# Fixed sets of PSUM banks for the feed-forward matmuls in place of a running count over seven banks

## The chip, the cores and the metric

The kernel runs on all eight cores of one Trainium2 chip. Each core runs the same program on its own four sequences of the batch and exchanges nothing with the others. The metric is the device time of the slowest core in microseconds (us).

## What is computed

The input x has 32 sequences of 2048 tokens with 1024 features. Three blocks follow one another, each on a layer norm of its input and each added to it: half of a gated feed-forward block, an attention-like block with a decaying running sum, and half of the same feed-forward block again.

```python
def ffn(x, w_gate, w_up, w_down):        # weights are int32, times 1/127
    gate = x @ (w_gate / 127).T          # 1024 -> 3072
    up   = x @ (w_up / 127).T            # 1024 -> 3072
    return (silu(gate) * up) @ (w_down / 127).T

x = x + 0.5 * ffn(layernorm(x), w_gate, w_up, w_down)
x = x + attn(layernorm(x), Wq, Wv, Wo, Wg, beta, ln_gamma, ln_beta)
x = x + 0.5 * ffn(layernorm(x), w_gate, w_up, w_down)
```

In `attn`, q, v and a gate are projections of x, the state is a running sum of v with one decay per head, q times the state is normalised, multiplied by silu of the gate, and projected with Wo.

## The kernel before, in words

**Order of the program.** The weights are first cast and transposed into scratch tensors in HBM (`prep_cast`, `prep_T_gu` L396 on, `prep_T_d`). Then, for each of the four sequences s = 0 to 3, come phase A (`ffn_phase`), phase B (`attn_phase`) and phase C (`ffn_phase` again). The attention weights are transposed by DMAs that the SyncE queue (SP) issues during the first phase A (`prep_T_attn`).

**A small scheduler.** The class `Em` records the instructions of each engine in the order of the code and works out the semaphore waits from names of resources. It never reorders anything. Each PSUM bank is one such name (`PSB0` to `PSB6`). `group` records the eight matmuls that accumulate into one bank; the first of them waits until whoever last read that bank is done. So the order of work is the order of the code, and which earlier read a matmul waits for is set by the bank number alone.

**PSUM.** `PSB[0]` to `PSB[6]` are seven banks of 128x512 fp32; an eighth, `PSB7`, holds transposes.

**`ffn_phase`.** It begins with a layer norm (`layer_norm_to_xn`): for each of 16 chunks of 128 tokens, VectorE normalises (L566), TensorE transposes eight 128x128 blocks into PSB7 (L570), ScalarE copies them to XN (L576). The hidden dimension of 3072 is worked in three slabs j = 0, 1, 2 of 1024. In each slab there are five passes over TensorE, one after the other:

- gate, first half (hs = 0): 16 groups of 8 matmuls (L610), each group read out of its bank by ScalarE with Silu into SG (L627);
- up, first half: 16 groups (L638), each read out by VectorE, which multiplies by SG into H (L648);
- gate, second half, and up, second half, in the same way (hs = 1);
- down: 32 groups (L664), two for each chunk c of 128 tokens, read out in slab 0 by ScalarE (L674) and in slabs 1 and 2 by VectorE, which adds them to ACC (L678).

In slab 2, after the two groups of a chunk, VectorE adds ACC to X (L684). In phase A it then also sums the chunk for the next layer norm (`ln_stats`, L541, with a square on ScalarE, L545).

**The tail of phase C.** There `boundary_cb` is called for each chunk. After chunks 3, 7, 11 and 15 it stores a quarter of X (L911) and loads the same quarter of the next sequence over it (L916), both on the GpSimd queue (POOL). After chunks 7, 11 and 15 it also puts the four sums (L541) of the quarter loaded before into VectorE's queue, which wait for that load. The last quarter's sums come behind the phase.

**Banks.** One counter `pbc` runs through all passes of a phase, and each group takes the next of seven banks. In phase B the three projections of a chunk (`proj`, L722) take banks 4, 5 and 6 in turn and are read out by ScalarE (L735, L744, L749).

```python
bank = pbc[0] % 7        # in each of the three passes
pbc[0] += 1
```

Of the kernel before, what the change touches and what calls it, by code (L numbers as in the profile page):

```python
# [246 lines left out]
def build_program():  # L247
# [331 lines left out]
    def ffn_phase(tap=False, prestats=True, next_stats=True, tail_cb=None,  # L579
                  skip_gw0=False):  # L580
        layer_norm_to_xn(prestats=prestats)
        if tap:
            em.dma("st", lambda g: g.dma_start(out=dbg_xn, in_=XN[:]),
                   reads=[k for row in kXN for k in row], writes=["DBGXN"])
        nsl = NSLAB if DBG_SLABS is None else DBG_SLABS
        pbc = [0]
        for j in range(nsl):
            li = 3 * j
            slots = [(WA, "WSLOTA"), (WB, "WSLOTB")]
            wg_sl, wg_k = slots[li % 2]  # L590
            wu_sl, wu_k = slots[(li + 1) % 2]
            wd_sl, wd_k = slots[(li + 2) % 2]
            if not (skip_gw0 and j == 0):
                em.dma("wl", lambda s, a=wg_sl, j=j: s.dma_start(
                    out=a[:].rearrange("p (k h) -> p k h", h=SLAB), in_=scr_g[:, j]),
                    reads=[f"scrT_wgate_r{r}" for r in range(HID // 128)], writes=[wg_k])
                em.dma("wl", lambda s, a=wu_sl, j=j: s.dma_start(
                    out=a[:].rearrange("p (k h) -> p k h", h=SLAB), in_=scr_u[:, j]),
                    reads=[f"scrT_wup_r{r}" for r in range(HID // 128)], writes=[wu_k])
            if tap and j == 0:  # L600
                em.dma("st", lambda g, a=wg_sl: g.dma_start(out=dbg_wa, in_=a[:]),
                       reads=[wg_k], writes=["DBGWA"])
            for hs in range(2):
                for g in range(4):
                    for m4 in range(4):
                        m = 4 * hs + m4
                        bank = pbc[0] % 7
                        pbc[0] += 1
                        items = [(lambda t, k=k, m=m, g=g, wg_sl=wg_sl, bank=bank:
                                  t.matmul(PSB[bank][:],  # L610
                                           wg_sl[:, SLAB * k + 128 * m:SLAB * k + 128 * (m + 1)],
                                           XN[:, S * k + 512 * g:S * k + 512 * (g + 1)],
                                           start=(k == 0), stop=(k == KC - 1)),
                                  [wg_k] + [kXN[k][4 * g + i] for i in range(4)])
                                 for k in range(KC)]
                        em.group("tensor", items, writes=[kPSB[bank]])
                        if tap and j == 0 and hs == 0 and g == 0 and m4 == 0:
                            dps = HF[:, 4096:4608]
                            em.op("vector", lambda v, bank=bank: v.tensor_copy(
                                dps, PSB[bank][:]),  # L620
                                reads=[kPSB[bank]],
                                writes=[kH[4][i] for i in range(4)], war=B_H)
                            em.dma("st", lambda g2: g2.dma_start(out=dbg_ps, in_=dps),
                                   reads=[kH[4][0]], writes=["DBGPS"])
                        dst = SG[:, S * m4 + 512 * g:S * m4 + 512 * (g + 1)]
                        em.op("scalar", lambda s, dst=dst, bank=bank:
                              s.activation(dst, PSB[bank][:], AF.Silu,  # L627
                                           scale=np32(1.0 / 127.0)),
                              reads=[kPSB[bank]], writes=[kSG[m4][g]],
                              war=["WGT"] + PREP_SG_KEYS)  # L630
                for g in range(4):
                    for m4 in range(4):
                        m = 4 * hs + m4
                        hc = m
                        bank = pbc[0] % 7
                        pbc[0] += 1
                        items = [(lambda t, k=k, m=m, g=g, wu_sl=wu_sl, bank=bank:
                                  t.matmul(PSB[bank][:],  # L638
                                           wu_sl[:, SLAB * k + 128 * m:SLAB * k + 128 * (m + 1)],
                                           XN[:, S * k + 512 * g:S * k + 512 * (g + 1)],  # L640
                                           start=(k == 0), stop=(k == KC - 1)),
                                  [wu_k] + [kXN[k][4 * g + i] for i in range(4)])
                                 for k in range(KC)]
                        em.group("tensor", items, writes=[kPSB[bank]])
                        dst = H[:, S * hc + 512 * g:S * hc + 512 * (g + 1)]
                        src0 = SG[:, S * m4 + 512 * g:S * m4 + 512 * (g + 1)]
                        em.op("vector", lambda v, dst=dst, src0=src0, bank=bank:
                              v.tensor_tensor(dst, src0, PSB[bank][:], ALU.mult),  # L648
                              reads=[kSG[m4][g], kPSB[bank]], writes=[kH[hc][g]],
                              war=B_H)  # L650
            if tap and j == 0:
                em.dma("st", lambda g: g.dma_start(out=dbg_sg, in_=SG[:]),
                       reads=ALL_SG, writes=["DBGSG"])
                em.dma("st", lambda g: g.dma_start(out=dbg_h, in_=H[:]),
                       reads=ALL_H, writes=["DBGH"])
            em.dma("wl", lambda s, a=wd_sl, j=j: s.dma_start(
                out=a[:].rearrange("p (k h) -> p k h", h=D), in_=scr_d[:, j]),
                reads=[f"scrT_wdown_s{j}r{r}" for r in range(D // 128)], writes=[wd_k])
            for c in range(NCH):
                for n in range(2):  # L660
                    bank = pbc[0] % 7
                    pbc[0] += 1
                    items = [(lambda t, hc=hc, c=c, n=n, wd_sl=wd_sl, bank=bank:
                              t.matmul(PSB[bank][:],  # L664
                                       H[:, S * hc + 128 * c:S * hc + 128 * (c + 1)],
                                       wd_sl[:, D * hc + 512 * n:D * hc + 512 * (n + 1)],
                                       start=(hc == 0), stop=(hc == 7)),
                              [wd_k, kH[hc][c // 4]])
                             for hc in range(8)]
                    em.group("tensor", items, writes=[kPSB[bank]])  # L670
                    dst = ACC[:, D * c + 512 * n:D * c + 512 * (n + 1)]
                    if j == 0:
                        em.op("scalar", lambda s, dst=dst, bank=bank:
                              s.activation(dst, PSB[bank][:], AF.Copy, scale=SFIN),  # L674
                              reads=[kPSB[bank]], writes=[kACC[c][n]], war=WAR_ACC_A)
                    else:
                        em.op("vector", lambda v, dst=dst, bank=bank:
                              v.scalar_tensor_tensor(dst, PSB[bank][:], SFIN, dst,  # L678
                                                     ALU.mult, ALU.add),
                              reads=[kPSB[bank], kACC[c][n]], writes=[kACC[c][n]])  # L680
                if j == NSLAB - 1 or (DBG_SLABS is not None and j == DBG_SLABS - 1):
                    xc = X[:, D * c:D * (c + 1)]
                    ac = ACC[:, D * c:D * (c + 1)]
                    em.op("vector", lambda v, xc=xc, ac=ac: v.tensor_tensor(  # L684
                        xc, xc, ac, ALU.add),
                        reads=[kX[c], kACC[c][0], kACC[c][1]], writes=[kX[c]])
                    if next_stats:
                        ln_stats(c)
                    if tail_cb is not None:
                        tail_cb(c)  # L690
        if tap:
            em.dma("st", lambda g: g.dma_start(out=dbg_acc, in_=ACC[:]),
                   reads=ALL_ACC, writes=["DBGACC"])
# [289 lines left out]
```

How the kernel before makes its waits and increments, by code:

```python
        def body(engobj, eng):  # L225
            waited = {}
            for inst in em.ins[eng]:
                for dep in inst["deps"]:
                    sem, val = resolve(dep)
                    key = id(sem)
                    if waited.get(key, 0) < val:
                        engobj.wait_ge(sem, val)
                        waited[key] = val
                bi = inst["fn"](engobj)
                if inst["stream"] is not None:
                    bi.then_inc(semh[("d", inst["stream"])], 16)
                elif inst["inc"]:
                    bi.then_inc(semh[("e", eng)], 1)
```

## Time and profile before

| | us |
|---|---|
| Time, median of two runs | 7798.15 |
| The two runs | 7376.51 and 8219.79 |
| The profiled execution: its own time | 7241.5 |
| Its span (slowest core, core 1) | 7240.0 |
| Shortest span of a core (core 2) | 7209.6 |
| PE busy (share of the span) | 5696.3 (79%) |
| DVE busy | 2079.6 (29%) |
| ACT busy | 1474.6 (20%) |
| POOL busy | 173.1 (2%) |

PE is TensorE's matmuls, PEld its weight loads, DVE VectorE, ACT ScalarE, POOL GpSimd and SP SyncE. A matmul's row lasts from its start to its modelled end. Matmuls overlap in the pipeline, so the distance from one start to the next is shorter than a row. "Idle before" is the idle time of an engine ahead of an instruction, and the arrow names what ended it. PEclk is the granted clock of TensorE as a share of full speed.

### The profile page before, as it was taken

What the parts mean: (1) busy time and instruction counts of PE and PEld (TensorE: products, weight loads), DVE (VectorE), ACT (ScalarE), POOL (GpSimd) and SP (SyncE); (2) the same over time, 40 slices, a digit from 0 to 9 for tenths busy, and PEclk for the clock granted to TensorE, in tenths of its full rate; (3) what the DMA queues carried; (4) which work ended last, traced back from release to release, by engine and by line L of the source; (5) the groups of instructions that cost most, each with busy time, mean ns of one, the idle gap of its engine ahead of it and who ended that gap; (6) DMA issues with size and microseconds to landing.
All of it is one profiled execution on the core that took longest, in us unless ns stands there. A gap on an engine that the chain in (4) does not pass through costs nothing.

```text
span 7240.0 us, 81303 instructions; the slowest of 8 cores (7209.6 to 7240.0 us)
## 1 busy us (share of the span) xinstructions
PE 5696.3 (79%) x29138; PEld 2832.0 (39%) x29138; DVE 2079.6 (29%) x3929; ACT 1474.6 (20%) x2342; POOL 173.1 (2%) x112
## 2 busy tenths in 40 slices
PE   1012999686998799786998799786999799786899
PEld 0011444343443344443443344443444344443444
DVE  0012124244123213344123213444123213444123
ACT  1000212222211211322211221322211221322211
POOL 0000000000000000000000000000000000000000
PEclk9999999787999899887999899887999799887999
DMA  8733013200013000100013110100013110100001
GB/s 99 116 95 98 24 47 78 75 1 24 24 47 98 31 36 24 47 1 24 24 47 84 40 40 24 47 1 24 24 38 86 41 47 24 47 1 24 24 36 70
DMA packets 152527, 322.14 MB, mean 44 GB/s; under 512 B 112336, under 2 KB 112336, under 8 KB 140048
## 3 DMA queue, kind: packets, MB, share of 16 engines
q1 hardware_dynamic: 134016, 239.10, 10.0%
q0 software_dynamic: 18128, 77.84, 6.3%
q8 instruction: 253, 4.15, 0.2%
q14 instruction: 130, 1.06, 0.1%
HBM read 291.74 MB, written 88.08 MB: 52 GB/s over the span
## 4 chain that ended last, share of the span: by engine, by line
PE 70%; DVE 9%; DMA 8%; issue 5%; ACT 4%; another core or an unknown queue 3%; DVEq 1%; SPq 0%; ACTq 0%; POOL 0%; POOLq 0%
PE PSB L610 19%; PE PSB L638 18%; PE PSB L664 14%; PE PSB L722 9%; PE PSB L850 5%; PE PSB7b L570 2%; ACT XN L576 2%; DMA TSTB<-nat_g 2%; DMA o<-X 1%; DVE ACC L678 1%; DMA TSTB<-nat_u 1%; DVE STATS L541 1%; ACT ACC L843 1%; PE PSB7b L839 1%
## 5 line engine op out<-in xcount | busy, mean ns | idle before, releaser
L648 DVE TENSOR_TENSOR H<-SG,PSB 128x512 bf16<-128x512 bf16 x768 | 527.7, 687 | 2621.4 <-PE PSB L638 2621.4
L627 ACT ACTIVATE SG<-PSB 128x512 bf16<-128x512 f32 x768 | 458.5, 597 | 2200.7 <-PE PSB L610 2200.7
L610 PE MATMUL PSB<-XN,WA 128*128 128x512 bf16 x4096 | 902.9, 383 | 0.0
L664 PE MATMUL PSB<-WA,H 128*128 128x512 bf16 x4096 | 888.6, 379 | 6.7 <-DVE ACC L678 6.7
L638 PE MATMUL PSB<-XN,WB 128*128 128x512 bf16 x4096 | 889.3, 379 | 0.0
L610 PEld LDWEIGHTS PSB<-XN,WA 128*128 128x128 bf16 x4096 | 404.4, 99 | 491.5 <-issue 18.0
L664 PEld LDWEIGHTS PSB<-WA,H 128*128 128x128 bf16 x4096 | 400.8, 98 | 491.8 <-issue 10.1
L638 PEld LDWEIGHTS PSB<-XN,WB 128*128 128x128 bf16 x4096 | 400.6, 98 | 483.5
L570 PE MATMUL PSB7b<-IDN,TMPTM 128*128 128x128 bf16 x1536 | 194.0, 305 | 498.9 <-ACT XN L576 268.0
L545 ACT ACTIVATE TMPTM<-X 128x1024 bf16<-128x1024 bf16 x192 | 202.8, 1056 | 1192.7 <-DMA X<-x 496.6
L678 DVE SCALAR_TENSOR_TENSOR ACC<-PSB,ACC 128x512 bf16<-128x512 f32 x512 | 350.3, 689 | 329.4 <-PE PSB L664 327.1
L610 PE MATMUL PSB<-XN,WB 128*128 128x512 bf16 x2048 | 444.6, 379 | 0.0
L638 PE MATMUL PSB<-XN,WA 128*128 128x512 bf16 x2048 | 444.6, 379 | 0.0
L664 PE MATMUL PSB<-WB,H 128*128 128x512 bf16 x2048 | 443.3, 379 | 0.0
L405 PE MATMUL PSB7b<-IDN,TSTB 128*128 128x128 bf16 x384 | 48.6, 306 | 481.5 <-DMA TSTB<-nat_g 353.0
L850 PE MATMUL PSB<-ACC 128*128 128x512 bf16 x1024 | 347.3, 514 | 87.2 <-ACT ACC L843 87.2
L570 PEld LDWEIGHTS PSB7b<-IDN,TMPTM 128*128 128x128 bf16 x1536 | 148.3, 137 | 547.1 <-issue 547.1
L576 ACT ACTIVATE XN<-PSB7b 128x1024 bf16<-128x1024 bf16 x192 | 196.6, 1024 | 810.6 <-PE PSB7b L570 810.6
L839 PE MATMUL PSB7b<-IDN,ACC 128*128 128x128 bf16 x512 | 63.9, 304 | 315.3 <-DVE ACC L835 315.3
L610 PEld LDWEIGHTS PSB<-XN,WB 128*128 128x128 bf16 x2048 | 200.5, 98 | 241.5
L664 PEld LDWEIGHTS PSB<-WB,H 128*128 128x128 bf16 x2048 | 200.4, 98 | 241.6
L638 PEld LDWEIGHTS PSB<-XN,WA 128*128 128x128 bf16 x2048 | 200.3, 98 | 241.7
(95 smaller groups left out, 4017.3 us busy)
## 6 DMA issues: line engine op xcount, KB each, us to landing
WA<-scr_g SPq DMA_DIRECT2D x16, 2048.0 KB, 7.8
WB<-scr_u SPq DMA_DIRECT2D x16, 2048.0 KB, 7.8
WA<-scr_d SPq DMA_DIRECT2D x16, 2048.0 KB, 7.5
o<-X POOLq DMA_DIRECT2D x16, 2048.0 KB, 8.3
X<-x POOLq DMA_DIRECT2D x16, 1024.0 KB, 10.8
WB<-scr_g SPq DMA_DIRECT2D x8, 2048.0 KB, 7.3
WA<-scr_u SPq DMA_DIRECT2D x8, 2048.0 KB, 7.5
WB<-scr_d SPq DMA_DIRECT2D x8, 2048.0 KB, 7.5
```

What stands on the lines that cost most here:

```text
L545: s.activation(sq, xc, AF.Square, accum_out=stat("ssq", c)),
L570: items = [(lambda t, tm=tm, f=f, bank=bank: t.transpose(bank[:, 128 * f:128 * (f + 1)], tm[:, 128 * f:128 * (f + 1)], IDN[:]), [f"TT{c % ...
L576: em.op("scalar", lambda s, xnv=xnv, bv=bv: s.activation(xnv, bv, AF.Copy), reads=[bkey], writes=[kXN[f][c] for f in range(KC)])
L610: t.matmul(PSB[bank][:], wg_sl[:, SLAB * k + 128 * m:SLAB * k + 128 * (m + 1)], XN[:, S * k + 512 * g:S * k + 512 * (g + 1)], start=(k == ...
L627: s.activation(dst, PSB[bank][:], AF.Silu, scale=np32(1.0 / 127.0)),
L638: t.matmul(PSB[bank][:], wu_sl[:, SLAB * k + 128 * m:SLAB * k + 128 * (m + 1)], XN[:, S * k + 512 * g:S * k + 512 * (g + 1)], start=(k == ...
L648: v.tensor_tensor(dst, src0, PSB[bank][:], ALU.mult),
L664: t.matmul(PSB[bank][:], H[:, S * hc + 128 * c:S * hc + 128 * (c + 1)], wd_sl[:, D * hc + 512 * n:D * hc + 512 * (n + 1)], start=(hc == 0) ...
L678: v.scalar_tensor_tensor(dst, PSB[bank][:], SFIN, dst, ALU.mult, ALU.add),
L722: t.matmul(PSB[bank][:], XN[:, S * k + 128 * c:S * k + 128 * (c + 1)], wslot[:, D * k + 512 * n:D * k + 512 * (n + 1)], start=(k == 0), st ...
L839: items = [(lambda t, y2=y2, f=f, bank=bank: t.transpose(bank[:, 128 * f:128 * (f + 1)], y2[:, 128 * f:128 * (f + 1)], IDN[:]), [kY2C[sl], ...
L850: t.matmul(PSB[bank2][:], Y2FM[sl][:, 128 * k:128 * (k + 1)], WOT[:, D * k + 512 * n:D * k + 512 * (n + 1)], start=(k == 0), stop=(k == KC ...
```

## The change

The counter goes. A group's bank now comes from its place in its pass: gate and up groups take banks 0 to 2 by (4g + m4) mod 3, down groups take banks 3 to 6 by (2c + n) mod 4. Nothing else is changed, and no instruction changes its place on its engine.

```diff
-        pbc = [0]
         for j in range(nsl):
...
             for hs in range(2):
                 for g in range(4):
                     for m4 in range(4):
                         m = 4 * hs + m4
-                        bank = pbc[0] % 7
-                        pbc[0] += 1
+                        bank = (g * 4 + m4) % 3
...
                 for g in range(4):
                     for m4 in range(4):
                         m = 4 * hs + m4
                         hc = m
-                        bank = pbc[0] % 7
-                        pbc[0] += 1
+                        bank = (g * 4 + m4) % 3
...
             for c in range(NCH):
                 for n in range(2):
-                    bank = pbc[0] % 7
-                    pbc[0] += 1
+                    bank = 3 + (c * 2 + n) % 4
```

The next two pieces are TensorE's instructions at the seam between the first gate pass and the first up pass of a phase. `XN,WA` are gate groups, `XN,WB` up groups, and PSB with its number is the bank. First as before:

```order
L610 MATMUL PSB0<-XN,WA 128x512 [waits se_scalar,se_tensor]
L610 MATMUL PSB0<-XN,WA 128x512 x7
L610 MATMUL PSB1<-XN,WA 128x512 [waits se_scalar,se_tensor]
L610 MATMUL PSB1<-XN,WA 128x512 x7
L638 MATMUL PSB2<-XN,WB 128x512 [waits sd_wl,se_scalar,se_tensor]
L638 MATMUL PSB2<-XN,WB 128x512 x7
L638 MATMUL PSB3<-XN,WB 128x512 [waits se_scalar,se_tensor]
L638 MATMUL PSB3<-XN,WB 128x512 x7
```

And now, on the same engine and at the same place:

```order
L608 MATMUL PSB2<-XN,WA 128x512 [waits se_scalar,se_tensor]
L608 MATMUL PSB2<-XN,WA 128x512 x7
L608 MATMUL PSB0<-XN,WA 128x512 [waits se_scalar,se_tensor]
L608 MATMUL PSB0<-XN,WA 128x512 x7
L635 MATMUL PSB0<-XN,WB 128x512 [waits sd_wl,se_scalar,se_tensor]
L635 MATMUL PSB0<-XN,WB 128x512 x7
L635 MATMUL PSB1<-XN,WB 128x512 x8
L635 MATMUL PSB2<-XN,WB 128x512 x8
```

Before, the first up group takes the bank after the last gate group's. Now the last gate group and the first up group share bank 0, and the two groups behind them wait for nothing.

The third place is the start of a down pass on TensorE (`WA,H` are down groups), first before, then now.

```order
L638 MATMUL PSB0<-XN,WB 128x512 [waits se_tensor,se_vector]
L638 MATMUL PSB0<-XN,WB 128x512 x7
L664 MATMUL PSB1<-WA,H 128x512 [waits sd_wl,se_tensor,se_vector]
L664 MATMUL PSB1<-WA,H 128x512 x7
L664 MATMUL PSB2<-WA,H 128x512 [waits se_tensor,se_vector]
L664 MATMUL PSB2<-WA,H 128x512 x7
```

Now it is:

```order
L635 MATMUL PSB0<-XN,WB 128x512 [waits se_tensor,se_vector]
L635 MATMUL PSB0<-XN,WB 128x512 x7
L660 MATMUL PSB3<-WA,H 128x512 [waits sd_wl]
L660 MATMUL PSB3<-WA,H 128x512 x7
L660 MATMUL PSB4<-WA,H 128x512 x8
L660 MATMUL PSB5<-WA,H 128x512 x8
L660 MATMUL PSB6<-WA,H 128x512 x8
L660 MATMUL PSB3<-WA,H 128x512 [waits se_scalar,se_tensor]
```

The down pass begins in banks that the up pass doesn't use, and comes back to its first bank after four groups instead of seven.

## Rows read from the trace of the kernel before

**Rows 1.** The page: the chain that ended last, by engine and by line.
```profile
PE 70%; DVE 9%; DMA 8%; issue 5%; ACT 4%; another core or an unknown queue 3%; DVEq 1%; SPq 0%; ACTq 0%; POOL 0%; POOLq 0%
PE PSB L610 19%; PE PSB L638 18%; PE PSB L664 14%; PE PSB L722 9%; PE PSB L850 5%; PE PSB7b L570 2%; ACT XN L576 2%; DMA TSTB<-nat_g 2%; DMA o<-X 1%; DVE ACC L678 1%; DMA TSTB<-nat_u 1%; DVE STATS L541 1%; ACT ACC L843 1%; PE PSB7b L839 1%
```
**Rows 2.** The chain in order of time, a slab: start, us, what.
```profile
1827.60 29.23 PE PSB L610 x128
1856.82 27.63 PE PSB L638 x128
...
1939.70 55.25 PE PSB L664 x256
```
**Rows 3.** Who waited for whom: total us, times, longest.
```profile
PE PSB L664 <- DVE ACC L678: 6.7, 3, 3.0
```
**Rows 4.** Timeline at a seam: start, us, engine, line, count [idle before <-releaser].
```profile
774.34 4.05 PE L638 MATMUL PSB<-XN,WB 128*128 128x512 bf16 x18
774.60 0.60 ACT L627 ACTIVATE SG<-PSB 128x512 bf16<-128x512 f32 x1 [1.13 <-PE PSB L610]
776.34 0.69 DVE L648 TENSOR_TENSOR H<-SG,PSB 128x512 bf16<-128x512 bf16 x1 [35.60 <-PE PSB L638]
```
**Rows 5.** Timeline, weight transposes: one bank, read by DVE.
```profile
641.49 0.69 DVE L438 COPY SG<-PSB7b 128x1024 bf16<-128x1024 bf16 x1 [1.33 <-PE PSB7b L430]
642.33 1.01 PE L430 MATMUL PSB7b<-IDN,SG 128*128 128x128 bf16 x8 [1.01 <-DVE SG L438]
```
**Rows 6.** Timeline, layer norm: one bank, read by ACT.
```profile
2375.30 1.02 ACT L576 ACTIVATE XN<-PSB7b 128x1024 bf16<-128x1024 bf16 x1 [1.46 <-PE PSB7b L570]
2376.68 1.01 PE L570 MATMUL PSB7b<-IDN,TMPTM 128*128 128x128 bf16 x8 [1.48 <-ACT XN L576]
```
**Rows 7.** Timeline of PE in phase B, projections in three banks.
```profile
1385.38 3.62 PE L722 MATMUL PSB<-WB,XN 128*128 128x512 bf16 x16
...
1395.73 1.45 PE L758 MATMUL PSB<-H,LBUF 128*128 128x64 f32 x12
```
**Rows 8.** Timeline, last down pass of the first phase A, PE and DVE.
```profile
1188.74 55.42 PE L664 MATMUL PSB<-WA,H 128*128 128x512 bf16 x256
...
1243.54 1.42 DVE L678 SCALAR_TENSOR_TENSOR ACC<-PSB,ACC 128x512 bf16<-128x512 f32 x2
```
**Rows 9.** The chain in order of time, end of the first phase A.
```profile
1133.65 27.64 PE PSB L610 x128
1161.78 8.02 DMA TSTB<-nat_wq
```
**Rows 10.** Timeline of PE, down passes at the tails of phase C, s = 0, then s = 1.
```profile
2271.06 53.82 PE L664 MATMUL PSB<-WA,H 128*128 128x512 bf16 x248
2326.61 1.89 PE L664 MATMUL PSB<-WA,H 128*128 128x512 bf16 x8 [1.72 <-DVE ACC L678]
...
3944.43 13.97 PE L664 MATMUL PSB<-WA,H 128*128 128x512 bf16 x64 [1.93 <-DVE ACC L678]
3961.40 3.17 PE L664 MATMUL PSB<-WA,H 128*128 128x512 bf16 x8 [3.00 <-DVE ACC L678]
```
**Rows 11.** Timeline of DVE at the tails of s = 0 (first five), s = 1, s = 2.
```profile
2310.08 1.28 DVE L678 SCALAR_TENSOR_TENSOR ACC<-PSB,ACC 128x512 bf16<-128x512 f32 x2
...
2317.45 0.69 DVE L684 TENSOR_TENSOR X<-X,ACC 128x1024 bf16<-128x1024 bf16 x1
2320.32 2.54 DVE L541 TENSOR_REDUCE STATS<-X 128x1 f32<-128x1024 bf16 x2 [2.18 <-DMA X<-x]
...
2325.78 1.28 DVE L678 SCALAR_TENSOR_TENSOR ACC<-PSB,ACC 128x512 bf16<-128x512 f32 x2
...
2333.14 0.69 DVE L684 TENSOR_TENSOR X<-X,ACC 128x1024 bf16<-128x1024 bf16 x1
...
3955.47 5.19 DVE L541 TENSOR_REDUCE STATS<-X 128x1 f32<-128x1024 bf16 x4 [3.80 <-DMA X<-x]
...
5585.08 5.19 DVE L541 TENSOR_REDUCE STATS<-X 128x1 f32<-128x1024 bf16 x4 [0.75 <-DMA X<-x]
```

## The prediction

> **What bounds the kernel now.** I read the chain of work that ended last first, since it says whose delay is the kernel's delay. TensorE holds 70% of it, and its three largest lines are the feed-forward matmuls: gate L610 19%, up L638 18%, down L664 14% [rows 1]. The chain in order of time shows how tight they are: in one slab the passes of 128, 128, 128, 128 and 256 matmuls stand end to end with nothing between them [rows 2]. A pass of 128 takes 27.63 us, so one matmul of 512 columns every 27.63 / 128 = 0.216 us, and a group of eight every 1.727 us. Only the first pass of a phase is longer. So anything that stops TensorE inside a feed-forward phase is paid in full. The list of waits then says that TensorE hardly ever waits for a bank there: three waits, 6.7 us together [rows 3]. The change can only add such waits, or leave things as they are.
>
> **Steady state, inside a pass.** With three banks a group waits for the read-out of the group three before it. At the seam of the first gate and up pass, the last gate matmul starts 0.216 us before 774.34, at 774.12. ScalarE begins to read 0.48 us after that start and takes 0.60; VectorE's first read of an up group, at 776.34, begins 0.49 us after the last matmul of its group starts (774.34 + 7 x 0.216 = 775.85) and takes 0.69 [rows 4]. Both are over 1.2 us after the group's last matmul started, and the bank is wanted again only after two more groups, 3.45 us. Price: nothing. The same arrangement already runs: in phase B the projections turn over three banks with ScalarE reading, and six groups start at 1385.38 and are over at 1395.73, 1.725 us each [rows 7]. The down passes have four banks, so still more room. In the last slab of phase A VectorE is nearly full. The last matmul of down group 30 starts at 1188.74 + 31 x 1.727 - 0.22 = 1242.06, so its read could begin at 1242.55 and begins at 1243.54 [rows 8]: a lag of 1.0 us. Four banks allow 3 x 1.727 + 0.22 less the turn-round of 0.49 + 0.69 + 0.15, or 4.1 us. Price nothing.
>
> **The seams between passes.** A gate or up pass has 16 groups, and 15 mod 3 = 0: its last group sits in bank 0, and so does the first group of the next gate or up pass. That group must wait until the last one has been computed and read out. The distance that was seven groups is one. There are three such seams in a slab (gate to up, up to gate, gate to up); up to down goes from bank 0 to bank 3, down to gate from bank 6 to bank 0, and both are free. Three seams by three slabs by eight phases make 72: 48 behind a ScalarE read, 24 behind a VectorE read.
>
> Price of one, from start of the last matmul to start of the next, less the 0.216 us that it takes now:
> - ScalarE: 0.48 until the read begins, 0.60 for the read [rows 4], and from the end of a ScalarE read to TensorE's next start 2376.68 - (2375.30 + 1.02) = 0.36 [rows 6]. Sum 1.44, less 0.22: 1.22 us.
> - VectorE: 0.49, 0.69 [rows 4], and from the end of the read to the next start 642.33 - (641.49 + 0.69) = 0.15 [rows 5]. Sum 1.33, less 0.22: 1.11 us.
>
> The trace before shows no such wait at full clock with a 128x512 read-out, so I bound it. The nearest VectorE row has TensorE idle for 1.01 us [rows 5]; take 0.9 as the lower end for both. The ScalarE row idles 1.48 us for a read that is 0.42 us longer [rows 6]; with a full 1.48 as upper end the read would gain nothing from being short. I take the sums worked out above, since each part has its own row.
>
> Do the seams lie on the path? All but one: the first phase A leaves TensorE's chain at 1161 us, after its last gate pass, for the DMAs that transpose the attention weights [rows 9], so its last seam is covered; without that cover it would cost 1.2 us more. Seams: 47 x 1.22 + 24 x 1.11 = 57.3 + 26.6 = 84 us.
>
> **The tails of phase C.** Here VectorE stands still behind sums that wait for loads of the next sequence, and the number of banks says how far TensorE may run ahead. At s = 0 the down pass starts at 2271.06 [rows 10], so group 20 is due at 2271.06 + 20 x 1.727 = 2305.6. With four banks it needs VectorE's read of group 16, which begins at 2310.08 and takes 0.64 [rows 11], and 0.15 for the turn: 2310.9, a stop of 5.3 us where there was none. At s = 1 TensorE already stopped 1.93 us, at group 23 [rows 10]; three banks fewer stop it three groups sooner, 1.93 + 3 x 1.73 = 7.1 us. At s = 2 it didn't stop, so the new stop is at most 5.2 us.
>
> Most of that is taken back, because VectorE, with its backlog, and the loads set the end of this tail. Such a stop will halve TensorE's clock for a while: behind an idle of 3.00 us eight matmuls took 3.17 us, behind 1.72 only 1.89 [rows 10]. I give it 2 us. Then at s = 0 group 23 starts at 2310.9 + 3 x 1.73 + 2 = 2318.1, its read begins 2.0 us later, and read and addition end some 1.5 after that: chunk 11 is added at 2321.6 instead of 2317.45 + 0.69 = 2318.1 [rows 11], 3.5 us late. Behind it VectorE idled for the next load 2.18, 3.80 and 0.75 us at s = 0, 1, 2 [rows 11], which covers part of it: 1.3, 0 and 2.8 us are left. Then the sums end, VectorE reads group 24, and TensorE may start group 28; group 31 is computed, read and added after 0.79 + 4 x 1.73 - 0.22 + 0.49 + 1.5 = 9.5 us, where VectorE alone needed 2333.83 - 2325.78 = 8.05 [rows 11]: 1.4 us more at each. Tails: 2.7 + 1.4 + 4.2 = 8.3 us. Below, they could cost 3 if the clock stays up; above, 15 if the later stores and loads collide. The fourth sequence has no load behind it and no such tail.
>
> **Sum.** 84 + 8.3 = 92.3 us, on the profiled execution's own 7241.5: 7334 us, 1.3% more. That execution lies 7.1% below the median shown, and 1.8% below the lower of its two runs. I forecast for an execution like the profiled one. By the bounds, seams 71 x 0.9 = 64 to 71 x 1.48 = 105 and tails 3 to 15 give 67 to 120: 7308 to 7362.
>
> **The rivals.**
> *The clock falls at the seams.* If an idle of 1 us in an otherwise full pass took TensorE from 2.4 to 1.2 GHz, each seam would also pay a climb back; the first pass of a phase, behind the layer norm, is 29.23 - 27.63 = 1.6 us longer than the next [rows 2]. 71 x 1.6 = 114 us more: 7448 us, 2.9% slower. Against it: behind idles of 1.72 and 1.93 us the matmuls ran at full pace at once (8 in 1.89 us, 64 in 13.97), and only the idle of 3.00 us was followed by half pace [rows 10]. The seams idle about 1.05. For it: those two came once each, not every 28 us. It decides from some 33 of the 71 seams on, where 92 + 33 x 1.6 passes 2%.
> The Trainium skill, "TensorE: Matmul & The Clock Gate", section "A second HAM failure mode: psum-queue depth-cycling", speaks against this change: in a kernel that cycled through banks, "the PE micro-idles between MM groups frequently enough that HAM oscillates", and throughput suffers. By that rule the time would be that rival's; the rows of 1.72 and 1.93 us speak for the other, so it keeps a small chance.
>
> *Three banks hold up every group.* If a near wait cost each of the 2304 groups (288 in each of eight phases) even the 0.15 us from the end of a read to TensorE's start [rows 5], that is 346 us more: 7680 us, 6% slower. Against it stand the projections, which run in three banks at full pace [rows 7].
>
> *The change doesn't cost what it says.* If the seams were covered as the one at the end of the first phase A is, only the tails would be left: 7250 us. For it speaks only that DMAs and VectorE hold 17% of the chain; against it, that the passes with the seams stand end to end on it [rows 2].
>
> **How the numbers follow.** Forecast 0.81; clock at the seams 0.09; every group 0.02; nothing at the seams 0.08. Its own range is 7308 to 7362; to hold 8 in 10 I reach below to 7290, for seams cheaper than any row, and above past the clock rival to 7460. Beyond 2% (145 us, about what a measurement of this kernel tells from no change), slower has the clock rival, the group rival and a few hundredths of the forecast's own spread: 0.14. Faster has no mechanism at all, only scatter: 0.02. Within 2%: 0.84.
>
> **What would show it.** In the profile after, the list of waits should have TensorE's up pass waiting for ScalarE's Silu read 48 times, about 1.0 to 1.1 us each, and its gate pass waiting for VectorE's read 24 times, about 1.0; in the chain, the passes should still take 27.6 us each, with about 1.2 between them. At the tails TensorE should wait 5 to 7 us for VectorE once in each of the first three phases C, and again 1 to 2 us. Passes of 29 us behind the seams would mean the clock; gaps inside passes, the second rival; a single wait per seam of over 1.5 us, that my turn-round is too short. Line numbers after the change are a few lower.

## The result, and the profile after

The changed kernel is slower by the ratio 1.0126, with a 95% interval of 1.0096 to 1.0155. The profiled execution takes 7330.68 us where the one before took 7241.5, 89.2 us more; the forecast was 92.3 us more and a ratio of 1.013. The median over the eleven runs taken, however, is 7659.26 us (7326.11 to 8276.72), and that of ten runs before 7636.82 us. In some executions of either kernel the cores of one die or both are granted a lower clock and need some per cent longer, so the ratio and all comparisons below are made without them. The range of the forecast, 7290 to 7460, doesn't hold that median.

The chain that ended last, by engine and by line, in the page of the changed kernel:

```profile
PE 69%; DVE 9%; DMA 8%; issue 5%; ACT 5%; another core or an unknown queue 3%; DVEq 1%; SPq 0%; ACTq 0%; POOL 0%; POOLq 0%
PE PSB L608 18%; PE PSB L635 18%; PE PSB L660 14%; PE PSB L718 9%; PE PSB L846 5%; PE PSB7b L570 2%; ACT XN L576 2%; DMA TSTB<-nat_g 2%; DMA TSTB<-nat_u 1%; DVE STATS L541 1%; DVE ACC L674 1%; DMA o<-X 1%; ACT ACC L839 1%; DMA X<-x 1%
```

It is the same chain as in [rows 1]. ScalarE has gone from 4% to 5%; its reads at the seams now stand in it. The list of waits of the changed kernel shows where (who waited for whom, total us, times, longest):

```profile
PE PSB L635 <- ACT SG L625: 48.1, 48, 1.2
PE PSB L608 <- DVE H L645: 23.7, 24, 1.0
PE PSB L660 <- DVE ACC L674: 17.2, 6, 6.8
```

Up groups wait for ScalarE's read of the last gate group 48 times, gate groups for VectorE's read of the last up group 24 times, each about 1.0 us. Neither line was there before. The third line answers to [rows 3]: six waits instead of three.

The same seams in the chain in order of time (start, us, what), in the slab that answers to [rows 2]:

```profile
1864.89 6.06 PE PSB L608 x28
1870.94 0.02 issue
1870.96 0.02 ACTq L232
1870.98 0.04 issue
1871.03 0.61 ACT SG L625
1871.63 0.24 issue
1871.87 27.80 PE PSB L635 x128
1899.67 0.03 issue
1899.70 0.02 DVEq L232
1899.72 0.04 issue
1899.77 0.70 DVE H L645
1900.47 0.14 issue
1900.60 4.48 PE PSB L608 x20
```

Between two passes the chain leaves TensorE, goes through one read, and comes back. I call this way, from the last matmul of a group to the first of the next group in the same bank, the turn-round. A pass itself is as long as before: 27.80 us is the old 27.63 with the last matmul's way through the pipeline, which nothing overlaps any more. From the start of this up pass to the start of the gate pass behind it are 28.73 us, 1.10 more than 27.63; the next up pass starts at 1929.39, 28.79 later, 1.16 more.

TensorE in the down passes at the tails of phase C, s = 0, 1 and 2 (start, us, instruction, count, idle before and releaser):

```profile
2333.54 15.25 PE L660 MATMUL PSB<-WA,H 128*128 128x512 bf16 x64 [3.33 <-DVE ACC L674]
2350.27 7.07 PE L660 MATMUL PSB<-WA,H 128*128 128x512 bf16 x32 [1.48 <-DVE ACC L674]
...
3988.83 15.34 PE L660 MATMUL PSB<-WA,H 128*128 128x512 bf16 x64 [6.75 <-DVE ACC L674]
4004.70 7.07 PE L660 MATMUL PSB<-WA,H 128*128 128x512 bf16 x32 [0.53 <-DVE ACC L674]
...
5645.91 16.23 PE L660 MATMUL PSB<-WA,H 128*128 128x512 bf16 x64 [4.59 <-DVE ACC L674]
5662.66 7.07 PE L660 MATMUL PSB<-WA,H 128*128 128x512 bf16 x32 [0.53 <-DVE ACC L674]
```

They answer to [rows 10]. Each tail now has one long stop and one short one. How long differs from core to core: over the eight cores the long ones are 2.8 to 5.8, 4.2 to 6.8 and 2.7 to 4.7 us at s = 0, 1 and 2. Behind the long ones, 64 matmuls took 15.25, 15.34 and 16.23 us, where they took 13.97 in [rows 10]: 1.3 to 2.3 us go to half clock (PEclk is 0.62 and 0.56 on average in the first 3 us or so behind the stops at s = 0 and 1). Behind the short ones 32 matmuls took 7.07 us, full pace.

To see past single cores, whose tails differ by some microseconds, I took on every core the start of the first gate matmul of each phase, and the mean over the cores of the time from one to the next. The last phase C, which has no border, went from 510.5 to 520.8 us: 10.3 for nine seams, 1.14 each. A phase C with a border went from 582.8 to 596.4, 13.6 more, so 3.4 beyond its nine seams. Phases A and B together went from 1048.5 to 1059.4 for the later three sequences and from 1079.4 to 1090.3 for the first, 10.9 more in both.

### The profile page after: what moved, and what is told of

It is laid out like the page before. It is cut to its first block, busy times and chain, and to the rows that moved or that the text cites. A ratio compares the mean times of both kernels' runs of the same rounds, so it can differ in the third digit from the quotient of the medians.

```text
span 7328.9 us, 80815 instructions; the slowest of 8 cores (7303.7 to 7328.9 us)
## 1 busy us (share of the span) xinstructions
PE 5714.8 (78%) x29138; PEld 2828.3 (39%) x29138; DVE 2081.3 (28%) x3929; ACT 1474.7 (20%) x2342; POOL 173.0 (2%) x112
## 4 chain that ended last, share of the span: by engine, by line
PE 69%; DVE 9%; DMA 8%; issue 5%; ACT 5%; another core or an unknown queue 3%; DVEq 1%; SPq 0%; ACTq 0%; POOL 0%; POOLq 0%
PE PSB L608 18%; PE PSB L635 18%; PE PSB L660 14%; PE PSB L718 9%; PE PSB L846 5%; PE PSB7b L570 2%; ACT XN L576 2%; DMA TSTB<-nat_g 2%; DMA TSTB<-nat_u 1%; DVE STATS L541 1%; DVE ACC L674 1%; DMA o<-X 1%; ACT ACC L839 1%; DMA X<-x 1%
## 5 line engine op out<-in xcount | busy, mean ns | idle before, releaser
L835 PE MATMUL PSB7b<-IDN,ACC 128*128 128x128 bf16 x512 | 63.3, 302 | 315.3 <-DVE ACC L831 315.3
```

## The experiments

All are edits of the kernel before. A "die's span" is the median of its four cores, and where there are several dies, the median of those. For the kernel before this is 7220.7 us, on the chip and at the time of the runs on the seams, the tails, the sums and the transposes. The three runs with one or two banks came from another chip; the kernel before took 7231.0 us at best beside them, and they are compared with that. Each of the three rests on one execution. "More" and "less" for the mean of a phase are against the profiled execution of the kernel before.

**The seams alone.** The change's banks for gate and up, seven banks for down.

```diff
-                        bank = pbc[0] % 7          # gate and up
-                        pbc[0] += 1
+                        bank = (g * 4 + m4) % 3
...
-                    bank = pbc[0] % 7              # down
-                    pbc[0] += 1
+                    bank = (3 + c * 2 + n) % 7
```

> Gate and up groups in banks 0 to 2 by their place in the pass, as in the change, so that the last group of one pass and the first of the next share bank 0; the down groups run over all seven banks, starting at bank 3. Theory (seams cost a turn-round each, tails little): the 72 waits at the seams stay, about 1.0 us of idle each, and the stops of 3 to 7 us in the down passes of phase C are gone. Own time of the profiled execution 7241 + 71 x 1.13 = about 7321 us. Rival (tails carry most): 7241 + 5 to 15 = about 7250. Rival (the clock falls at the seams): 7440 and more, with gate and up passes longer than 27.8 us.

Measured: a die's span of 7302.0 us, the median of seven dies, 81.3 more than before. The fastest run took 7317.7 us; an interval for the ratio isn't on record. The waits on core 1:

```profile
PE PSB L636 <- ACT SG L626: 47.7, 48, 1.0
PE PSB L609 <- DVE H L646: 23.7, 24, 1.0
```

No down group waits. The forecast for the seams was 84 us. The seams make nine tenths of the loss. The clock rival is out: gate and up passes behind a seam take 27.80 us, as in the changed kernel.

**The tails alone.** Three banks for gate and up by a count that runs on, four for down.

```diff
-                        bank = pbc[0] % 7          # gate and up
+                        bank = pbc[0] % 3
...
-                    bank = pbc[0] % 7              # down
-                    pbc[0] += 1
+                    bank = 3 + (c * 2 + n) % 4
```

> The gate and up groups turn over three banks by a count that runs on from pass to pass, so that no two neighbours share a bank; the down groups keep the change's four banks. Theory: no wait at a seam, gate and up passes of 27.63 us end to end; TensorE stops 3 to 7 us once in each of three tails of phase C, and the own time is 7241 + 4 to 10 = 7245 to 7251 us. Rival (three banks are too few in themselves): waits inside or between passes and 7300 us or more.

Measured: ratio 1.0022, interval 0.9975 to 1.007; a die's span of 7229.6 us, 8.9 more than before. The chain on core 7, a slab:

```profile
1820.30 29.22 PE PSB L610 x128
1849.53 27.63 PE PSB L638 x128
1877.15 27.63 PE PSB L610 x128
1904.78 27.63 PE PSB L638 x128
1932.41 55.25 PE PSB L663 x256
```

This is [rows 2] again, with three banks. A phase C with a border takes 585.8 us on average, 3.0 more than before, the last one 510.4. So four banks cost only at the borders, some 9 us in all, which the interval of the ratio alone wouldn't tell from nothing, and three banks cost nothing where neighbours don't share one. The two parts add up to 81.3 + 8.9 = 90.2 us. Between the two profiled executions lie 89.2 us by their times, and 93 us by the medians of their dies (7224.4 and 7317.6).

**Two banks.** As the seams run, but gate and up groups alternate over two banks.

```diff
+                        bank = pbc[0] % 2          # gate and up, running on
...
+                    bank = (3 + c * 2 + n) % 7     # down
```

> Gate and up groups turn over only two banks, by a count that runs on over the passes, so each group takes the bank of the group two before; down groups run over seven banks from bank 3. Theory (what costs is distance one alone, since the turn-round less a matmul, 1.1 to 1.2 us, fits into the 1.73 us of one group between): no wait, passes of 27.63 us, own time 7241 us within 0.3%. Rival (fewer banks cost in themselves, and three was already near the edge): waits at each of the 1536 gate and up groups, 0.1 us each would be 150 us, 7390 us or more.

Measured: 7230.0 us in the profiled execution, against 7231.0. The chain:

```profile
1873.09 27.63 PE PSB L610 x128
1900.72 27.63 PE PSB L638 x128
```

No gate or up group waits. Even two banks are enough for TensorE to run on. What costs is distance one (the next group takes the same bank), not the number of banks.

**One bank for the up passes.** Distance one inside a pass, VectorE reading.

```diff
+                        bank = 1 + (g * 4 + m4) % 2   # gate
...
+                        bank = 0                      # up
...
+                    bank = (3 + c * 2 + n) % 7        # down
```

> All up groups in bank 0, gate groups alternate over banks 1 and 2, down groups over seven banks from bank 3: no shared bank at a seam, but 15 shared banks inside each of 48 up passes, read by VectorE. Theory (a turn-round of 1.10 us each with the clock up): 720 waits of 0.99 us, an up pass takes 27.6 + 15 x 1.10 = 44.1 us, own time 7241 + 48 x 16.5 less at most 16 hidden in the first phase A = 8017 to 8033 us. Rival (an idle of 1 us every 2.8 us takes the clock down): an up pass of 16 groups at 0.43 us a matmul, 54.6 + 15 x 1.1 = 71 us, own time 9300 us.

Measured: 8045.58 us in the profiled execution, 815 more than 7231.0. TensorE in an up pass of slab 0, then of slab 1:

```profile
1942.01 1.89 PE L636 MATMUL PSB<-XN,WB 128*128 128x512 bf16 x8 [0.94 <-DVE H L646]
1944.84 1.89 PE L636 MATMUL PSB<-XN,WB 128*128 128x512 bf16 x8 [0.94 <-DVE H L646]
...
2214.05 1.89 PE L636 MATMUL PSB<-XN,WA 128*128 128x512 bf16 x8 [1.01 <-DVE H L646]
2216.94 1.89 PE L636 MATMUL PSB<-XN,WA 128*128 128x512 bf16 x8 [1.01 <-DVE H L646]
```

Groups start 2.83 us apart in slab 0, 1.10 more than 1.73, as forecast, but 2.90 us apart in slabs 1 and 2, 1.17 more. With 240 waits at 1.10 and 480 at 1.17, less the 16.8 us by which the wait for the attention weights shrank on core 1 (33.9 to 17.1 us), the sum is 809 us, beside 815 measured. The expected 8017 to 8033 us were too low because 480 turn-rounds took 0.07 us more than the 1.10 expected, 34 us. And the clock stays up although TensorE stands still a third of the time:

```profile
1930.00:1960.00 30.00, 23.41 (x105) 9.57 (x104) 4.82 (x7) 3.59 (x6) 0.00 (x0) 1.00 0.00 1
```

This is a stretch of 30 us, most of it in such a pass: PE busy 23.41, PEclk (third from the end) 1.00.

**One bank for the gate passes.** The same with ScalarE reading.

```diff
+                        bank = 0                      # gate
...
+                        bank = 1 + (g * 4 + m4) % 2   # up
...
+                    bank = (3 + c * 2 + n) % 7        # down
```

> The same for the gate passes, read by ScalarE: all gate groups in bank 0, up groups alternate over banks 1 and 2. Theory (a turn-round through ScalarE is 1.16 us, with 0.24 from the end of the read to TensorE's start, as at the changed kernel's seams): 720 waits of 1.00 us, a gate pass 27.6 + 15 x 1.16 = 45.0 us, own time 7241 + 48 x 17.4 = 8076 us. Rival (0.36 from read to start, as in the layer norm): 1.28 us each, 8160 us. Rival (the clock falls): 9300 us.

Measured: 8072.56 us in the profiled execution, 842 more. The waits, on core 5:

```profile
PE PSB L609 <- ACT SG L626: 722.6, 720, 2.3
```

That is 842 / 720 = 1.17 us for a turn-round through ScalarE, with an idle of 1.00. Groups start 2.88 or 2.89 us apart in nearly all passes, 1.16 more than 1.73, as expected; longer gaps in the first pass of a phase make up the rest. The wait for the attention weights isn't shorter here (34.0 us on core 5, where it was 34.1), so nothing is hidden. The rival with the 0.36 us of the layer norm is out: it had 8160 us.

**The sums behind the phase.** The kernel before, with VectorE's sums for the next sequence moved out of the down pass.

```diff
-                if q >= 1:
-                    for i in range(4):
-                        ln_stats(4 * (q - 1) + i)
...
-                for i in range(4):
-                    ln_stats(12 + i)
+                for i in range(16):
+                    ln_stats(i)
```

> The kernel before with seven banks, but the sums of the next sequence (line 541, and their squares on ScalarE) no longer stand between the chunks of the last down pass: all 16 chunks are summed behind the phase. Theory (those sums make VectorE stand still, which stops TensorE and delays the last store): no wait of TensorE for VectorE in a down pass, the last quarter's store is issued 3 to 9 us earlier at each of three borders, 16 sums of 1.3 us fit beside the last store and load except for the last four; own time 7241 - 10 to 18 = 7223 to 7231 us. Rival (the sums were hidden and now stand on the path): 3 x 12 x 1.3 = 47 us more, 7288 us.

Measured: ratio 1.0005, interval 0.998 to 1.003; a phase C with a border takes 580.9 us on average, 1.8 less than before. The tail of s = 0 on core 1: TensorE's down pass, then the chain.

```profile
2261.54 55.42 PE L664 MATMUL PSB<-WA,H 128*128 128x512 bf16 x256
```
```profile
2319.11 18.50 DMA o<-X
2338.14 11.10 DMA X<-x
```

TensorE is never stopped, and the last store goes out 2319.11 - 2261.54 = 57.6 us after the pass begins, where it was 2334.39 - 2271.06 = 63.3. But the store then takes 18.50 us instead of 15.71, and the load behind it 11.10 instead of 9.88. The third quarter's load was issued at 2315.81, 3.3 us before the store; before, the two were 6.8 us apart. Of 5.7 us gained 1.7 are left at this border. In a die's span, 7220.3 us against 7220.7, even that hardly shows. Neither number of the expectation came: the sums weren't hidden work that now stands on the path, and an earlier start of the last store comes through only in part. That store and load hold each other up is my reading of these times; no run separates it.

**Two banks for the transposes too.** The sums as above, and the layer norm's transposes alternate over the eighth bank and bank 6.

```diff
+    PSB6T = PSB[6][:].bitcast(BF16)
...
-            bank, bkey = PSB7, "PSB7"
+            bank, bkey = (PSB7, "PSB7") if c % 2 == 0 else (PSB6T, "PSB6")
```

> As the run with the sums behind the phase, and in the layer norm the transposes of even chunks go to the eighth bank and those of odd chunks to bank 6, so that neighbours don't share a bank. Theory (any group that takes the bank of its neighbour pays a turn-round; the layer norm pays it 15 times in each of 12 places): the idle of 1.48 us before each group of transposes goes, a chunk takes 1.1 to 1.4 us where it took 2.49, 12 x 15 x 1.1 to 1.4 = 200 to 250 us less, own time about 6980 to 7030 us. Rival (ScalarE's copy of 1.02 us or VectorE's normalisation sets the pace of a chunk in another way): 7150 to 7230 us.

Measured: ratio 0.9685 to the kernel before, interval 0.9653 to 0.9717; a die's span of 6995.3 us, 225 less than before, and as much less than with the sums moved alone. TensorE in a layer norm, where [rows 6] had one group and an idle of 1.48 us every 2.49:

```profile
1768.11 1.01 PE L571 MATMUL PSB7b<-IDN,TMPTM 128*128 128x128 bf16 x8 [0.62 <-ACT XN L577]
1769.02 1.01 PE L571 MATMUL PSB<-IDN,TMPTM 128*128 128x128 bf16 x8
1770.69 1.01 PE L571 MATMUL PSB7b<-IDN,TMPTM 128*128 128x128 bf16 x8 [0.66 <-ACT XN L577]
1771.51 1.05 PE L571 MATMUL PSB<-IDN,TMPTM 128*128 128x128 bf16 x8
```

Two chunks now take 2.5 to 2.6 us, 1.27 each, so 12 x 15 x 1.22 = 220 us are to be expected from these rows. This version is faster than both kernels.

## Why the prediction was right or wrong

**What bounds the kernel.** Right. What was put between the passes came out one for one in the time: 81.3 us for the seams, which stand end to end on the chain.

**Steady state.** Right, and with more room than claimed: two banks run at full pace, one doesn't.

**The seams.** Count and places right: 48 and 24 waits. The sum of 84 us measured 81.3, and that is closer than its terms were. The turn-round through VectorE was forecast at 1.11 us and is 1.10 in slab 0 but 1.17 in slabs 1 and 2, so it was put too low at most seams. The one through ScalarE was forecast at 1.22 and is 1.16, too high. The term of it that was off is the way from the end of ScalarE's read to TensorE's start: 0.36, taken from the transposes, against 0.24 in the chain here; the reason stands in the last section. The two errors partly cancel.

That the last seam of the first phase A is covered can't be seen in the changed kernel. The mean wait for the attention weights is 29.8 us before and 30.6 after, over cores that differ by 9 us and more, and the first phases A and B grew by 10.9 us like the later ones. The cover itself shows in the run with one bank for the up passes: there the mean wait is 12.8 us, 17.0 less, which is about one up pass of 15 turn-rounds of 1.17.

**The tails.** 8.3 us forecast, 8.9 in the run that has them alone. That there is one long stop in each tail, and that most of it is taken back, was right. The stops were 3.3, 6.8 and 4.6 us on the core of the page, against 5.3, 7.1 and at most 5.2. The first was forecast too long: VectorE comes back to the down groups 37.2 us after the down pass began (2332.71 - 2295.51), where it was 39.0 in the trace before (2310.08 - 2271.06), behind a load that lands at another moment on each core. As the stops differ by 2 to 3 us between cores, and the forecast had one core's rows, its closeness to 8.9 is partly luck.

**The rivals.** The rival of the clock at the seams fell: idles of 1.0 us leave it at 2.4 GHz, even every 2.8 us. On the cores that I read of the changed kernel and of the runs on seams, tails and banks, feed-forward matmuls at half pace stand only behind a layer norm and behind the long stops in the tails. The Trainium skill, "TensorE: Matmul & The Clock Gate", section "A second HAM failure mode: psum-queue depth-cycling", tells of a kernel in which micro-idles between groups made the clock oscillate; they don't here, at either spacing, and for this kernel the measurement decides. The rival that every group pays fell with the runs on three and two banks, and the one that nothing is paid with the seams alone.

**The time.** Here the forecast was wrong, though the difference was right. The step that failed is the base of the sum, 7241.5 us, and with it the range: "I forecast for an execution like the profiled one". The two runs then known, 7376.51 and 8219.79, both lay above it, by 1.9% and 13.5%, and I kept a range of 170 us, 7290 to 7460. In place of 7241.5 the median of ten runs of the kernel before is 7636.82, 395 us more, and the median of the changed kernel, 7659.26, lies 199 us above the range. The cause is the scatter common to both kernels, not the change: the medians stand as 1.003, the lowest times are 7240.16 and 7326.11, and each kernel scatters by some 1000 us. No run here was made to find what sets it. A range for the time, as against one for the difference, had to reach at least to the median shown with the effect added, 7798 + 1.3%.

## What to carry to other kernels

Ask of every PSUM bank which group used it last, also across loops: a modulus that starts afresh in each loop puts equal banks side by side wherever the length of the loop is one more than a multiple of it. Distance one costs a whole turn-round (1.1 to 1.2 us here for a 128x512 read), distance two (8 matmuls of 0.216 us between) already nothing; beyond that the number of banks mattered here only where the reader itself stood still for a time. And a price taken from one wait doesn't carry over to another before both have the same number of semaphore waits in front of them. The same look finds gains: the layer norm's single transpose bank cost this kernel over 200 us, 3%.

## What the runs showed that I had not expected

The same wait for the same VectorE read has two lengths, 0.94 us in slab 0 and 1.01 us in slabs 1 and 2, steady to a hundredth inside a pass. The read and the way back are equal in both, 0.69 and 0.15 us; the difference stands ahead of the read. The chain of that run shows it, in slab 0 and then in slab 1 (L232 is the line of the kernel that waits for a semaphore):

```profile
1946.74 0.03 issue
1946.77 0.02 DVEq L232
1946.79 0.04 issue
1946.84 0.70 DVE H L646
...
2215.95 0.03 issue
2215.97 0.02 DVEq L232
2215.99 0.05 issue
2216.04 0.02 DVEq L232
2216.06 0.04 issue
2216.11 0.70 DVE H L646
```

In slabs 1 and 2 the queue of VectorE runs two semaphore waits behind TensorE's last matmul instead of one, and the second takes 0.07 us. It is the same on ScalarE: a second wait moves its read from 0.48 to 0.53 us behind the start of the last matmul. It stands at 43 of the 48 seams behind ScalarE in the changed kernel, also at the one that costs 1.16 us in the chain above; with one wait such a seam costs 1.11.

The way from the end of a ScalarE read to TensorE's start is 0.24 us at the seams and 0.36 in the layer norm, and through VectorE 0.14 to 0.15. Here too it is the number of waits. These are the semaphore waits in TensorE's queue between the end of the read and the first matmul behind it: at a seam of the changed kernel, in the layer norm of the kernel before, and in an up pass of the run with one bank:

```profile
L232 PEldq EVENT_SEMAPHORE  x2: 51/51/51, 1871.7 to 1871.8; - x2
...
L232 PEldq EVENT_SEMAPHORE  x3: 51/51/51, 2376.4 to 2376.6; - x3
...
L232 PEldq EVENT_SEMAPHORE  x1: 51/51/51, 2219.7 to 2219.7; - x1
```

One, two and three waits go with 0.15, 0.25 and 0.36 us, 0.11 for each further one. The reading engine and the clock aren't needed to explain it: in phase B of the kernel before, the matmuls of L850 start 0.14 us behind a ScalarE read (L843) the 8 times that one wait stands between, and 0.25 the 56 times that two do. No run takes a single wait out to test it.

Taking TensorE's stops and 5.7 us of delay from the tail of phase C gave back only 1.8 us of a phase, as the store and load that end it grew longer.
